# Cross-attention and lookup-table FFN: small DVE steps of the first score stage moved to GpSimd, and the way from batch 0 to batch 1 written in another order

## The chip, the cores and the metric

One core of a Trainium2 chip runs the whole program. The metric is the device time of one launch in microseconds (us). Engines are named as the profile names them: PE (TensorE), DVE (VectorE), ACT (ScalarE), POOL (GpSimd) and SP (SyncE, which here only issues DMAs).

## What is computed

For four batches of 512 rows of 512 numbers: a layer norm, cross-attention with 16 heads against a context, and an FFN whose weights are picked from a table of 16 numbers by integer indices. Cut to what matters:

```python
q = _ln((x @ Wq + bq).reshape(b, s1, H, HD), qn_w, qn_b)        # H = 16 heads of HD = 32
k = _ln(y_main @ Wk + bk, kn_w, kn_b);  v = y_main @ Wv + bv      # 496 keys of the context
k_dca = _ln((y_dca @ Wkv_dca + bkv_dca)[:, :, 0], ...)            # its last 16 rows
ctx = softmax(q @ k.T / sqrt(HD)) @ v + softmax(q @ k_dca.T / sqrt(HD)) @ v_dca
x = x + ctx @ Wo + bo                                            # after _layernorm(x)
gate, up = lut[gate_idx] , lut[up_idx]                           # 1376 x 512 indices each
h = jax.nn.silu(x_ @ gate.T) * (x_ @ up.T)                       # x_ = _layernorm(x)
out = x + h @ lut[down_idx].T
```

Everything is kept to about float32: each operand is split into an fp16 high half and an fp16 low half (`low = value - high`), and a product is three matmuls (high*high, high*low, low*high).

## The kernel before, in words

Every engine has a program written out by hand; semaphores tie them together, so the order of an engine's work is the order in the code. A batch goes through `core(a, ...)` on each engine. Its parts are: projections and head norms of eight (batch 0: nine) **units**, each 128 rows of queries ("q") or keys ("k", "d"); a **score stage** of 32 steps `m`, taken in 16 pairs; a short **shift** part; and a **value stage** of 16 steps. Between the steps of one batch, `between(slot)` runs pieces of the FFN of the batch before. Batch 0 has no batch before it; its slots are used for building the FFN weights.

**Building the weights.** The indices come as int32. POOL casts them to fp16, one block at a time (`convert(it)`, line 586), SP stores a block to a DRAM copy (`store_idx`) and loads each of its 33 chunks back replicated (`load_rep(c)`, line 403, three buffers `l_rep`). DVE compares a chunk with four index values in four **comparisons** (`one_hot(c)`, line 1007, 128x2048 fp16, into `l_oh`, four quarters). PE multiplies these by the table (`look_up(c)`, line 1570), which leaves a high half in bank FB and a low half in bank FB + 1. ACT copies both out (`lookup_out(c)`, lines 722 and 723), after which `l_out` frees the banks. Chunks 0 to 15 are compared in the score stage of batch 0, one per pair, and the rest in its value stage; chunks 31 and 32 are looked up in the slots `AHEAD` and `AHEAD + 1`, that is, after batch 1 has begun.

**Score stage of batch 0.** For each step DVE takes a maximum over two heads (line 1308, from PSUM), ACT takes exponentials in place (line 895), and PE computes the next pair of scores (line 1794) into one of three pairs of banks. After the maxima of a pair DVE makes the four comparisons of a chunk, and PE looks up the chunk before. From the seventh pair on PE also projects a tile of values or keys of batch 1 per pair into the same bank FB + 1 (`early(e)`, line 1519), which ACT copies out (lines 750 and 753). For each of the four query tiles DVE also does three small steps on the 16 extra keys: `dca_top` (maximum, 1145), `dca_shift` (add the negated maximum, 1149) and `dca_sum` (1153), with ACT's exponential `dca_exp` (938) between the last two. Three more DVE steps stand in or next to this stage: `low_half(7)` and `low_half(8)` (line 1133) and `context_lo` (line 1084).

**From batch 0 to batch 1.** PE projects batch 1's remaining query tiles, turns normalised heads by transposes (`turn_heads(u)`, line 1716), and computes batch 0's output rows (`out_rows`). DVE adds the residual (`residual(t)`, line 1078) from `x2`, which SP loads from `x` (line 476). It then takes the moments, normalises (`standardise`) and splits off the low half (`stage`, line 1066). ACT's `stage` (line 740) makes the high half. SP turns both halves by transposing DMAs (`turn`, lines 435 and 437). The FFN of batch 0 begins on PE in slot 4 and waits until all eight have landed. `variance(u)` (1111), POOL's `rstd(u)` (638) and `normalise(u)` (1121) make the head norm of unit u, from ACT's `square(u)` (764).

**Memory.** `arena` is one tile that is cut again for each stage. In front of the change `x2` (residual) lies on the comparison quarters 2 and 3 (`oh_late`) and the first replica.

## Time and profile before

| what | value |
|---|---|
| device time, three runs | 828.86, 830.95, 832.27 us (median 830.95) |
| profiled execution | 831.39 us |
| its span | 829.6 us |
| mean granted clock of PE | 0.981 |
| busy: PE, DVE, ACT, POOL | 765.0, 520.6, 491.2, 234.6 us |
| score stage of batch 0 | from the first maxima at 60.02 us to about 146 us |
| value stage of batch 0 | about 149 to 207 us |
| from batch 0 to batch 1 | about 207 to 259.5 us, when PE begins batch 1's scores |

PE's busy share over the whole span is 92%, but it is not even: in 60 to 91 us it is 18.16 of 31 us. So the table has to be read by stage. Where DVE is busy without a break and the others wait for it, a step taken from DVE counts; where PE is busy without a break, only PE's work counts. The time of 831.39 us is that of the execution whose trace is read here; it lies 0.44 us above the median.

### The profile page before, as it was taken

What the parts mean: (1) busy time and instruction counts of PE and PEld (TensorE: products, weight loads), DVE (VectorE), ACT (ScalarE), POOL (GpSimd) and SP (SyncE); (2) the same over time, 40 slices, a digit from 0 to 9 for tenths busy, and PEclk for the clock granted to TensorE, in tenths of its full rate; (3) what the DMA queues carried; (4) which work ended last, traced back from release to release, by engine and by line L of the source; (5) the groups of instructions that cost most, each with busy time, mean ns of one, the idle gap of its engine ahead of it and who ended that gap; (6) DMA issues with size and microseconds to landing.
All of it is one profiled execution on the core that took longest, in us unless ns stands there. A gap on an engine that the chain in (4) does not pass through costs nothing.

```text
span 829.6 us, 14807 instructions
## 1 busy us (share of the span) xinstructions
PE 765.0 (92%) x5842; PEld 313.0 (38%) x5842; DVE 520.6 (63%) x1007; ACT 491.2 (59%) x1000; POOL 234.6 (28%) x248
## 2 busy tenths in 40 slices
PE   3777676899989999999999999999999999999998
PEld 1342222233434334223543343234533332255445
DVE  7879999899866995223759972218589911053211
ACT  3477888888535886663648876644578856511100
POOL 6782111000842222003642220005622210013320
PEclk9998999899989999999999999999999999999999
DMA  7739697396330000321300002232000000000001
GB/s 247 185 101 269 186 262 211 105 194 147 127 79 1 1 1 14 77 58 58 79 0 2 1 1 51 64 86 49 8 1 2 2 26 26 27 26 1 0 13 39
DMA packets 73252, 58.60 MB, mean 71 GB/s; under 512 B 33312, under 2 KB 60704, under 8 KB 73056
## 3 DMA queue, kind: packets, MB, share of 16 engines
q1 hardware_dynamic: 72848, 57.40, 26.3%
q8 instruction: 46, 0.75, 0.4%
q10 hardware_dynamic: 208, 0.26, 0.2%
q14 instruction: 22, 0.18, 0.1%
q0 software_dynamic: 128, 0.00, 0.0%
HBM read 41.72 MB, written 9.50 MB: 62 GB/s over the span
## 4 chain that ended last, share of the span: by engine, by line
PE 75%; DVE 16%; ACT 4%; issue 2%; DMA 1%; POOL 0%; SPq 0%; DVEq 0%; ACTq 0%
PE ps L1519 50%; PE ps L1840 7%; PE ps L1821 6%; PE ps L1570 5%; DVE nmax L1311 3%; DVE nmax L1312 3%; PE ps L1794 3%; DVE arena L1007 2%; PE ps L1827 2%; PE ps L1716 2%; DVE arena L1014 2%; DVE nmax L1308 1%; ACT ps L895 1%; DMA arena<-in_Wq 1%; ACT wf_hi L722 1%
## 5 line engine op out<-in xcount | busy, mean ns | idle before, releaser
L1519 PE MATMUL ps<-arena,wf_hi 128*128 128x512 f16 (+2 forms) x736 | 212.8, 373 | 4.1 <-DVE arena L1014 3.0
L895 ACT ACTIVATE ps<-ps,nmax 128x496 f32<-128x496 f32 x256 | 166.2, 652 | 26.8 <-DVE nmax L1311 26.8
L925 ACT ACTIVATE arena<-ps 128x1024 f32<-128x1024 f32 x128 | 124.3, 1026 | 74.0 <-PE ps L1827 74.0
L1519 PE MATMUL ps<-arena,wf_lo 128*128 128x512 f16 (+2 forms) x368 | 136.8, 372 | 0.0
L1519 PE MATMUL ps<-wf_hi,arena 128*128 128x512 f16 (+3 forms) x374 | 114.8, 368 | 0.0
L638 POOL TENSOR_TENSOR hrstd<-hvar,mhalf 128x16 f32<-128x16 f32 (+1 forms) x33 | 98.5, 3001 | 47.1 <-DVE hvar L1111 47.0
L1519 PEld LDWEIGHTS ps<-arena,wf_hi 128*128 128x128 f16 (+1 forms) x736 | 69.8, 100 | 91.7 <-DVE arena L1014 13.1
L1007 DVE TENSOR_SCALAR arena<-arena,wf_lo 128x2048 f16<-128x2048 f16 (+1 forms) x132 | 89.1, 738 | 4.4 <-PE ps L1570 4.3
L614 POOL TENSOR_TENSOR xrstd<-xvar,mhalf 128x1 f32<-128x1 f32 x32 | 20.4, 638 | 211.9 <-DVE xvar L1049 211.9
L1570 PE MATMUL ps<-arena,wf_lo 128*32 128x512 f16 (+1 forms) x1056 | 66.0, 391 | 8.6 <-ACT arena L750 2.7
L1519 PE MATMUL ps<-wf_lo,arena 128*128 128x512 f16 (+3 forms) x187 | 68.5, 366 | 0.0
L1840 PE MATMUL ps<-arena 128*32 128x512 f32 x512 | 68.2, 604 | 0.0
L1794 PE MATMUL ps<-arena 32*128 32x512 f16 x768 | 53.6, 382 | 12.1 <-ACT ps L895 12.1
L1519 PEld LDWEIGHTS ps<-wf_hi,arena 128*128 128x128 f16 (+1 forms) x374 | 36.4, 97 | 73.3 <-issue 38.8
L1312 DVE TENSOR_REDUCE nmax<-ps 128x1 f32<-128x496 f32 x96 | 63.8, 665 | 0.0
L1311 DVE TENSOR_REDUCE nmax<-ps 128x1 f32<-128x496 f32 x96 | 63.8, 665 | 0.0
L543 POOL TENSOR_TENSOR idle<-mhalf 128x1 f32<-128x1 f32 x44 | 8.9, 203 | 193.6 <-DVE arena L1022 193.6
L1027 DVE SCALAR_TENSOR_TENSOR arena<-ps,arena 128x512 f32<-128x512 f32 x15 | 10.4, 692 | 84.9 <-PE ps L1519 84.9
L730 ACT ACTIVATE arena<-ps 128x512 f32<-128x512 f32 (+1 forms) x44 | 26.3, 598 | 61.2 <-PE ps L1519 61.2
L1014 DVE SCALAR_TENSOR_TENSOR arena<-arena,ps 128x512 f32<-128x512 f32 (+1 forms) x44 | 30.0, 682 | 44.5 <-ACT arena L730 44.5
L1821 PE MATMUL ps<-arena 32*128 32x512 f16 x768 | 53.5, 381 | 0.0
L895 ACT ACTIVATION_READ_ACCUMULATOR ps<-ps,nmax 128x1 f32 x256 | 53.3, 208 | 0.0
(147 smaller groups left out, 1040.2 us busy)
## 6 DMA issues: line engine op xcount, KB each, us to landing
arena<-idx SPq DMA_DIRECT2D x124, 128.0 KB, 3.3
arena<-in_x SPq DMA_DIRECT2D x32, 256.0 KB, 2.9
wf_lo<-in_idx SPq DMA_DIRECT2D x10, 512.0 KB, 5.4
idx<-wf_hi SPq DMA_DIRECT2D x10, 384.0 KB, 3.5
out<-arena SPq DMA_DIRECT2D x15, 256.0 KB, 2.0
wf_lo<-in_idx SPq DMA_DIRECT2D x11, 256.0 KB, 6.2
arena<-in_ctxT SPq DMA_DIRECT2D x4, 512.0 KB, 5.0
arena<-in_Wq SPq DMA_DIRECT2D x4, 256.0 KB, 6.4
```

The source lines that it names most:

```text
L638: pool.tensor_tensor(hrstd[0:n_, u % 2, :], hvar[0:n_, u % 2, :], mhalf[0:n_, :], ALU.pow).then_inc(s["hrstd_set"], 1)
L895: last = act.activation(sc, sc, ACT.Exp, bias=nmax[:, 0, t, h:h + 1], accum_out=den[:, 0, t, h:h + 1])
L925: act.activation(probs[n_ % 2][:, 2 * p:2 * p + 2, :], ps[:, bank:bank + 2, :], ACT.Exp).then_inc(s["probs_set"], 1)
L1007: dve.tensor_scalar(l_oh[q][:, 0:n_], l_rep[c % REPS][:, 0:n_], l_j[:, q:q + 1], None, ALU.is_equal)\
L1014: dve.scalar_tensor_tensor(out=g, in0=g, scalar=1.0, in1=ps[0:m, ffn_bank(f, it), :], op0=ALU.add, op1=ALU.mult)\
L1311: dve.tensor_reduce(nmax[:, 0, t, 2 * p:2 * p + 1], sc[:, 0:1, DCA:S], AX_X, ALU.max, negate=True).then_inc(s["max_set"], 1)
L1312: dve.tensor_reduce(nmax[:, 0, t, 2 * p + 1:2 * p + 2], sc[:, 1:2, DCA:S], AX_X, ALU.max, negate=True)\
L1519: last = pe.matmul(dst, l, r, start=(first and i == 0), stop=(stop and i == len(todo) - 1))
L1570: last = pe.matmul(ps[g * 32:(g + 1) * 32, FB + a_, 0:w], l_c[a_][:, q, :], l_oh[q][:, g * w:(g + 1) * w], start=(q == 0), stop=(q == NJ - ...
L1794: last = pe.matmul(ps[:, pair_bank(m + j // 2) + j % 2, :], qT[x_][of_head(j), g, cols], kT[y_][of_head(j), g, :], start=(k == 0), stop=(k ...
L1821: pe.matmul(ps[:, SC + j, :], kT[x_][of_head(j), g, cols], qT[y_][of_head(j), g, :], start=(k == 0), stop=False)
L1840: last = pe.matmul(ps[j * HD:(j + 1) * HD, pv_bank(g), :], v_sb[:, kt, h * HD:(h + 1) * HD], probs[n_ % 2][:, j, :], start=(kt == 0), stop ...
```

## The change

1. **POOL takes small steps of DVE in batch 0's score stage.** `low_half(7)`, `low_half(8)`, the low half of the early context (in two halves) and the shifts `dca_shift` of tiles 0, 1 and 2 are done by POOL, each placed between casts and made to wait for a count of finished comparisons. The fourth shift stays on DVE.
2. **ACT** takes `dca_exp` one step later (p = 4) and DVE `dca_sum` two steps later (p = 7) in batch 0. `lookup_out` copies the low half first and announces it by a new semaphore `l_free`; `early` waits for that alone.
3. **PE** computes the first pair of scores before `turn_heads(8)`.
4. **Memory:** the replicas `l_rep` come first, so that `x2` lies on replicas 0 and 1. SP loads the residual when the comparisons of chunk 31 are done, ahead of its reload of the values, and no longer after the last look-up.
5. **From batch 0 to batch 1** the order on DVE, ACT, PE and POOL is written anew: the last chunk's comparisons are split in two pairs around the first residual, squares and variances come earlier, and PE begins the FFN (slot 4) before `turn_heads(5)`.

```diff
@@ memory
         at[0] = a_x
-        oh_late = [wide() for _ in range(2)]
         l_rep = [wide() for _ in range(2)]
-        l_oh = [wide() for _ in range(2)] + oh_late
+        l_oh = [wide() for _ in range(2)]
+        x_first = [xs[0], xs[1]] + [arena[:, at[0] + i * D:at[0] + (i + 1) * D] for i in range(2)]
+        l_oh += [wide() for _ in range(2)]
@@ SP
+            sp.wait_ge(s["oh_set"], NJ * (NCH - 1))
+            first = residual_row(0)
+            for t in range(T):
+                load_residual(t, first)
             sp.wait_ge(s["pv_done"], G * T)
             sp.wait_ge(s["v_out"], 16 * T)
             sp.dma_start(v_sb.rearrange("p t n -> p (t n)"), v_next).then_inc(s["v_in"], 16)
-            sp.wait_ge(s["oh_used"], NJ * NCH)
...
@@ POOL
+            def low_half(u):
+                t = UNITS_0[u][1]
+                cols = slice(t * P, (t + 1) * P)
+                pool.wait_ge(s["tr_lo"], u)
+                pool.wait_ge(s["tr_hi"], u + 1)
+                pool.tensor_tensor(qT[1][:, :, cols], ys[u % 2].rearrange("p (g s) -> p g s", g=G), qT[0][:, :, cols],
+                                   ALU.subtract).then_inc(s["tr_lo"], 1)
+            def context_low(chunks):
+                pool.wait_ge(s["oh_set"], NJ * chunks)
+                pool.wait_ge(s["cT_hi"], 2)
+                for k in range(KC):
+                    last = pool.tensor_tensor(cT_early[1][:, k, :], ctx_early[:, k * S:(k + 1) * S], cT_early[0][:, k, :], ALU.subtract)
+                last.then_inc(s["cT_lo"], 1)
+            def dca_shift(t, chunks):
+                part = sd[:, t * H:(t + 1) * H, :]
+                pool.wait_ge(s["oh_set"], NJ * chunks)
+                pool.wait_ge(s["dca_max"], t + 1)
+                pool.tensor_tensor(part, part, nmax[:, 1, t, :].unsqueeze(2).to_broadcast([P, H, DCA]), ALU.add).then_inc(s["sd_set"], 1)
...
@@ ACT
-                act.activation(wf_hi[:, lo:hi], ps[:, FB, 0:hi - lo], ACT.Copy)
-                act.activation(wf_lo[:, lo:hi], ps[:, FB + 1, 0:hi - lo], ACT.Copy).then_inc(s["l_out"], 1)
+                act.activation(wf_lo[:, lo:hi], ps[:, FB + 1, 0:hi - lo], ACT.Copy).then_inc(s["l_free"], 1)
+                act.activation(wf_hi[:, lo:hi], ps[:, FB, 0:hi - lo], ACT.Copy).then_inc(s["l_out"], 1)
...
-                    if p == 3 and t:
+                    if p == (4 if prev is None else 3) and t:
                         dca_exp(a, t - 1)
@@ DVE
+                    one_hot(NCH - 1, (0, 1))
+                    residual(0, prev)
+                    moments(2, 0, prev, rows_of(0))
+                    one_hot(NCH - 1, (2, 3))
...
-                    if m == 1:
+                    if m == 1 and prev is not None:
                         low_half(len(units) - 1)
-                    if t and p == 2:
+                    if t and p == 2 and prev is not None:
                         dca_shift(t - 1)
-                    if t and p == 5:
+                    if t and p == (7 if prev is None else 5):
                         dca_sum(t - 1)
...
-                if slot == S_ONE + 6:
-                    context_lo((0, 1), ctx_early, cT_early)
@@ PE
-                pe.wait_ge(s["l_out"], EARLY_FROM + e - 1)
+                pe.wait_ge(s["l_free"], EARLY_FROM + e - 1)
...
                     scores(m)
+                    if prev is None and m == 0:
+                        turn_heads(8)
```

On DVE, at the seventh and eighth step of batch 0's score stage (before), with the low half of the context between two maxima:

```order
L1308 TENSOR_REDUCE nmax<-ps 128x2
L1084 TENSOR_TENSOR arena<-arena 128x1024
L1308 TENSOR_REDUCE nmax<-ps 128x2
L1007 TENSOR_SCALAR arena<-arena,wf_lo 128x2048 x4
```

The steps that POOL does from the second cast on, in the kernel after (lines 632 low half, 639 context, 646 shift, 587 casts):

```order
L587 CAST wf_hi<-wf_lo 128x1536
L632 TENSOR_TENSOR arena<-arena 128x4x128
L587 CAST wf_hi<-wf_lo 128x1536 x2
L632 TENSOR_TENSOR arena<-arena 128x4x128
L587 CAST wf_hi<-wf_lo 128x1536
L639 TENSOR_TENSOR arena<-arena 128x512 x2
L587 CAST wf_hi<-wf_lo 128x1536
L646 TENSOR_TENSOR arena<-arena,nmax 128x256
L587 CAST wf_hi<-wf_lo 128x1536 x2
L646 TENSOR_TENSOR arena<-arena,nmax 128x256
L587 CAST wf_hi<-wf_lo 128x1536 x2
L646 TENSOR_TENSOR arena<-arena,nmax 128x256
```

Before, the casts stand there alone, one after the other; seven elementwise steps now stand among them.

PE from batch 0's last output rows to the first FFN pieces, before (1519 products, 1716 turned heads; the products with `wq` are the projections of units 5, 6 and 7):

```order
L1716 MATMUL ps<-ident,arena 128x128 x4
L1519 MATMUL ps<-wq,arena 128x512 x12
L1519 MATMUL ps<-b,sel_q 128x512
L1519 MATMUL ps<-wq,arena 128x512 x12
L1519 MATMUL ps<-b,sel_q 128x512
L1519 MATMUL ps<-wq,arena 128x512 x12
L1519 MATMUL ps<-b,sel_q 128x512
L1716 MATMUL ps<-ident,arena 128x128 x4
L1519 MATMUL ps<-arena,wf_hi 128x512 x2
```

and after (1552 products, 1749 turned heads):

```order
L1552 MATMUL ps<-wq,arena 128x512 x12
L1552 MATMUL ps<-b,sel_q 128x512
L1749 MATMUL ps<-ident,arena 128x128 x4
L1552 MATMUL ps<-wq,arena 128x512 x12
L1552 MATMUL ps<-b,sel_q 128x512
L1552 MATMUL ps<-wq,arena 128x512 x12
L1552 MATMUL ps<-b,sel_q 128x512
L1552 MATMUL ps<-arena,wf_hi 128x512 x2
```

Unit 5 is projected before unit 4 is turned, and the first FFN products (`wf_hi`) follow the last projection at once; the turning of unit 5 comes after the pieces of slot 4.

## Rows read from the trace of the kernel before

**Rows 1.** Busy time by engine in four stretches; then clock, DMA share, GB/s.

```profile
60.00:91.00 31.00, 18.16 (x232) 5.62 (x232) 30.43 (x39) 24.28 (x71) 5.88 (x4) 0.83 0.88 242
91.00:131.00 40.00, 31.90 (x358) 11.44 (x359) 38.77 (x51) 33.27 (x98) 4.88 (x4) 0.96 0.88 232
149.00:207.00 58.00, 57.83 (x855) 20.80 (x856) 52.98 (x93) 49.08 (x71) 2.22 (x4) 0.97 0.71 155
240.00:242.00 2.00, 0.00 (x0) 0.00 (x0) 0.28 (x1) 0.00 (x0) 2.00 (x2) 0.74 0.38 69
```

**Rows 2.** Timeline of DVE in the score stage: start, length, operation, idle before.

```profile
58.78 1.25 DVE L1133 TENSOR_TENSOR arena<-arena 128x512 f16<-128x512 f32 x1 [0.34 <-ACT arena L786]
60.02 2.29 DVE L1308 TENSOR_REDUCE nmax<-ps 128x2 f32<-128x992 f32 x2
62.23 0.68 DVE L1133 TENSOR_TENSOR arena<-arena 128x512 f16<-128x512 f32 x1
...
76.92 1.23 DVE L1084 TENSOR_TENSOR arena<-arena 128x1024 f16<-128x1024 f32 x1 [0.57 <-ACT arena L744]
...
95.43 2.74 DVE L1007 TENSOR_SCALAR arena<-arena,wf_lo 128x2048 f16<-128x2048 f16 x4 [0.27 <-PE ps L1570]
...
138.46 2.73 DVE L1007 TENSOR_SCALAR arena<-arena,wf_lo 128x2048 f16<-128x2048 f16 x4
...
144.41 0.42 DVE L1149 TENSOR_TENSOR arena<-arena,nmax 128x256 f32<-128x256 f32 x1
```

**Rows 3.** Operations by shape in 56 to 150 us: the shifts and the small maxima.

```profile
L1149 DVE TENSOR_TENSOR arena<-arena,nmax 128x256 f32<-128x256 f32 x4 | 3.0, 751 | 0.0
...
L1145 DVE TENSOR_REDUCE nmax<-arena 128x16 f32<-128x256 f32 x4 | 1.6, 408 | 0.0
```

**Rows 4.** Timeline of POOL: casts in the score stage, and a later low half.

```profile
58.02 1.47 POOL L586 CAST wf_hi<-wf_lo 128x1536 f16<-128x1536 int32 x1
65.63 1.47 POOL L586 CAST wf_hi<-wf_lo 128x1536 f16<-128x1536 int32 x1 [6.13 <-DVE arena L1007]
...
253.47 1.16 POOL L609 TENSOR_TENSOR arena<-arena 128x512 f16<-128x512 f32 x1
```

**Rows 5.** Chain of waits through one pair with an early projection: start, length.

```profile
96.65 0.60 ACT wf_hi L722
97.25 0.49 ACT wf_lo L723
...
97.79 1.48 PE ps L1519 x6
...
99.94 1.94 PE ps L1570 x32
```

**Rows 6.** Timeline of ACT: copying out an early value, an early key.

```profile
99.29 0.60 ACT L750 ACTIVATE arena<-ps 128x512 f32<-128x512 f32 x1 [0.16 <-PE ps L1519]
...
120.76 0.60 ACT L753 ACTIVATE arena<-ps 128x512 f32<-128x512 f32 x1 [0.38 <-PE ps L1519]
```

**Rows 7.** Chain of waits where the FFN of batch 0 begins.

```profile
238.43 4.08 issue
242.51 1.09 PE ps L1716 x4
243.60 4.73 PE ps L1519 x12
...
248.76 2.59 PE ps L1519 x12
```

**Rows 8.** Timeline of DVE there: the third residual.

```profile
228.99 0.68 DVE L1078 SCALAR_TENSOR_TENSOR arena<-ps,arena 128x512 f32<-128x512 f32 x1
```

**Rows 9.** Timeline of SP's queue: the last transposing DMAs; and their time to landing.

```profile
235.53 1.19 SPq L435 DMA_TRANSPOSE arena<-arena  x1
...
239.39 1.26 SPq L437 DMA_TRANSPOSE arena<-arena  x1
...
DMA to landing us min/median/max: 2.5/2.5/4.0
```

More of the change, by code:

```diff
@@ L485, in _ @@
             sp.dma_start(v_sb.rearrange("p t n -> p (t n)"), v_next).then_inc(s["v_in"], 16)
-            sp.wait_ge(s["oh_used"], NJ * NCH)
-            first = residual_row(0)
-            for t in range(T):
-                load_residual(t, first)
             def store(f, t):
@@ L652, in core @@
                     rstd(3)
+                    norm(2, 0, prev)
                     rstd(4)
-                    for t in range(T):
+                    for t in range(1, T):
                         norm(2, t, prev)
@@ L1481, in between @@
                 def between(slot):
-                    if not sum(f) and slot == AHEAD:
-                        one_hot(NCH - 1)
                     for it in range(IT):
@@ L1766, in core @@
                     project_values(4)
-                    for u in range(6, 9):
-                        turn_heads(u)
+                    turn_heads(6)
+                    turn_heads(7)
                 elif sum(a) > 1:
```

93 lines of the change are left out of this document (53 added, 40 removed).

## The prediction, before the kernel was run

> **What bounds the kernel now.** I read the busy times by stage first, because the shares over the whole span hide what matters. In 60 to 91 us DVE is busy 30.43 of 31 us and PE only 18.16; in 91 to 131 us DVE has 38.77 of 40 us; in 149 to 207 us PE has 57.83 of 58 us [rows 1]. So the first score stage is bound by DVE, its second half almost equally by something else, and the value stage behind it by PE, where nothing of this change can gain. Then I read DVE's timeline in the score stage. It is a plain alternation: two maxima (2.29 us in the row, the next step starts 2.21 us later), four comparisons (2.74 us, of which about 0.09 lies under the next step, so 2.65), and now and then an extra step [rows 2]. A pair of steps without extras is 2.20 + 2.65 = 4.85 us. The extras are what the change takes away. Then I read the chain of waits from 91 to 131 us. It does not stay on DVE: it runs look-up on PE (1.94), high half out (0.60), low half out (0.49), early projection on PE (1.48), copying that out on ACT (0.60), next look-up [rows 5, 6]. DVE waits for PE there, 0.27 us before the comparisons at 95.43 [rows 2]. Last, the chain of waits behind the value stage: PE stands still from 238.43 for 4.08 us, and what it does next, at 243.60, takes 4.73 us for the same 12 products that take 2.59 us at 248.76 [rows 7]. The granted clock falls in between (0.74 as a mean of 240 to 242 us, so it changed from the upper to the lower level near 241 us) [rows 1].
>
> **Start of the score stage.** Before, the first maxima start at 60.02, behind `low_half(7)`, which starts at 58.78 and takes 1.25 us, because POOL's cast from 58.02 to 59.49 runs beside it; the same step takes 0.68 us at 62.23 with no cast beside it [rows 2, 4]. Now POOL has that step, and PE computes the first scores before it turns unit 8. These scores need POOL's copies of the extra keys, which stand just before the cast at 58.02 [rows 4], so about 58.1; a first score pair is ready some 0.85 us later. I set the first maxima at 58.95: 1.07 us earlier.
>
> **First six pairs, up to the comparisons that started at 95.43.** Before that is 95.43 - 60.02 = 35.41 us [rows 2]. Now there are seven times two maxima (7 x 2.20), six times four comparisons (6 x 2.65) and one `dca_top` (the row says 408 ns, with its overlap taken off 0.33) [rows 3]: 15.40 + 15.90 + 0.33 = 31.63 us. The gain is 3.78 us. It checks against the parts: `low_half(8)` 0.60, `context_lo` 1.15 and its wait of 0.57, one shift 0.75 less its overlap, one `dca_sum` 0.33 that moves behind this point, and the wait of 0.27. With the start, the seventh chunk's comparisons begin 4.85 us earlier.
>
> **Next eight pairs, 95.43 to 138.46.** Before that is 43.03 us, two shifts among them; all four shifts average 751 ns but the one with no cast beside it takes 0.42 us [rows 2, 3]. DVE alone would now need 8 x 4.85 and four small steps of 0.33 = 40.1 us. The other loop needs more. In it ACT waits 0.16 us before it copies out an early value and 0.38 us before an early key [rows 6]; that is all that the low-half-first order can give, since ACT does the same two copies and the exponentials either way. From the end of one look-up to the end of the next is 0.03 + 0.60 + 0.49 + 0.05 + 1.48 + 0.02 + 0.61 + 0.04 + 1.94 = 5.26 us [rows 5, 6]; it becomes 5.10, and with keys, whose loop is 0.22 longer before, 5.10 too. `dca_exp`, moved to where ACT waits for the look-up, is hidden. Eight pairs of 5.10 are 40.8 us: 2.2 us less.
>
> **Taken off again.** POOL's new steps must fit beside the maxima. A low half costs POOL 1.16 us [rows 4]; the context is two such, 2.32; a shift is half the size and not shown on POOL, so its bounds are 0.58 (half of that row) and 1.16; I take 0.7. Each stands behind a count of comparisons, and the maxima last 2.20 us. Only one place overruns: cast and low half together are 1.47 + 1.16 = 2.63 us, 0.43 more than the two maxima. If the overrun stops the comparison it costs 0.43. Does a POOL step slow a maximum? The maxima beside the cast at 65.63 do not stretch: the second pair of DVE, 65.48 to 67.68, has the same 2.20 us. The bounds for the seven steps together are then 0 and 7 x 0.4 = 2.8 us (0.4 is what a cast costs a shift). I take 0.3, nearest to the row with the maxima.
> A rule of the Trainium skill speaks against the change here: "SBUF — State Buffer", section "Who interferes with whom", says that VectorE and GpSimd share a pair of ports as an exclusive lock, taken by a comparison of this kind (`tensor_scalar` in a two-port mode) or by two SBUF inputs against a GpSimd read, but never by a `tensor_reduce`. The stretched shifts and low half agree, and so do the unstretched maxima. By the rule the sum would lose the overrun of 0.43 us, by the rows 0.3.
> Score stage in all: 1.07 + 3.78 + 2.2 - 0.3 = 6.75 us. The value stage is PE work without a gap, so it only starts earlier and passes this on.
>
> **From batch 0 to batch 1** (times in the old clock of the trace). PE's work up to 238.43 is the same list in another order and has almost no gap before; I give it nothing. It resumes when the transposing DMAs have landed. Before, the third tile's first transpose starts at 235.53, the last at 239.39, and it lands 2.5 us after its start: 241.9 [rows 9]. PE resumed later still, at 242.51 [rows 7], for a head norm of unit 5. Now DVE's list up to the third residual is shorter in waits: the residual is loaded long before, and stepping the new order through with the row lengths (0.6 per 512-wide step, 1.32 for two comparisons, 1.1 for moments) puts that residual at about 227.0 where it was 228.99 [rows 8]. From there to the third tile's first transpose there are 5.7 to 6.5 us of steps, so it starts at 233 to 233.7, and the last landing is 6.4 us later, at 239.5 to 240.2. I take 240.1. The FFN pieces run first and `turn_heads(5)` behind them, with the same total, so PE is 242.51 - 240.1 = 2.4 us earlier. The head norm of unit 5 is ready at about 239.5 (variance 5 is taken before the last `stage`, some 2.9 us earlier) and the pieces cover it.
> The stop is then 238.4 to 240.1, shorter than the 2.6 us after which the clock fell. If the clock stays at 2.4 GHz, PE saves 4.73 - 2.59 = 2.14 us on the 12 products and, by the same factor 1.83, 0.5 to 0.65 us on the four transposes (1.09 us before): 2.8 us [rows 7]. Bounds: 0 and 2.8; I take 2.8, since the fall near 241 us lies behind the new start.
>
> **Cost at nothing, and its cover.** The residual's 1 MB now goes ahead of the reload of the values; that reload is first used by batch 1's value stage, over 100 us later. ACT's square of unit 5 waits for a projection of PE, but stands before a `stage` whose input comes later. DVE now waits for the last look-up before its first `standardise` of batch 0; queued behind it are the whole norm chain and the transposes. The look-up ends at about 222.8 and DVE gets there at about 223.4; if PE were later by more than 0.6 us, everything behind slides with it.
>
> **Sum.** 6.75 + 2.4 + 2.8 = 11.95 us off the profiled 831.39, which gives 819.4. That execution lies 0.44 above the median of 830.95, so against the median it would be 819.0. I predict 819.4, with its own range 817 to 822.
>
> **Rivals.**
> *The clock falls all the same* between the batches (the stop of PE is only shortened, to some 1.8 us, and a later landing lengthens it). Then the 2.8 us stay lost: 822.2. For it: the margin to 241 us is under 1 us. Against it: the fall came 2.6 us into the stop.
> *The replica loads take over in the score stage.* The DMA engines have a share of 0.88 at 242 GB/s in 60 to 91 us [rows 1]. The same bytes in 31 - 4.3 us would ask for 0.88 x 31 / 26.7 = 1.02. Against it: DVE waits for no load in the whole stage, and three replica buffers let a load be late by almost a pair. If it takes over, half of the 6.75 us goes: 822.8; with the clock falling too, 825.6.
> *POOL holds up the comparisons*: at its upper bound, 2.8 instead of 0.3 us, 821.9. For it: a cast beside a shift or a low half nearly doubled each [rows 2, 3]. Against it: the waits on counts keep all but one of POOL's steps beside maxima.
> *The gain is not there*: the chain in 91 to 131 us holds at its old 5.26 us a pair and more, and the order between the batches gives nothing, so only the first pairs gain: 831.4 - 4.5 = 826.9, within 0.5% of before.
> *Slower*: the early projections run at the lower clock. The first one already does so at 91 us, when PE has stood and waited. If PE stays at 1.2 GHz through the eight pairs, look-up and projection cost 1.6 and 1.2 us more (the 12 products of [rows 7] show a factor 1.83), a pair is 5.10 + 2.8 = 7.9 us, eight pairs lose 22.4 us, and the end is at 841.8. It outweighs all gains from the fifth such pair on. For it: PE is busy only 18.16 of 31 us before. Against it: the clock was 0.96 in 91 to 131 us, and PE has the same work in less time now.
>
> **Numbers.** Forecast 0.52, clock 0.16, loads 0.14, POOL 0.07, no gain 0.07, slower 0.04. A measurement of this kernel tells a change from none at about 0.5%, that is 4.2 us: under 826.8 is faster, over 835.1 slower. Faster is 0.52 + 0.16 + 0.14 + 0.07 = 0.89 and a part of the case without gain, 0.02; same 0.05; slower 0.04. The range for 8 in 10 is 815.5 to 826: it holds the forecast, the clock, loads and POOL, and below it a somewhat larger saving between the batches.
>
> **What would show it.** In the profile after: first maxima at about 59.0; pairs of 4.85 us up to the sixth comparison group, then 5.10, with DVE waiting for PE and the wait of ACT before lines 750 and 753 gone; the last comparisons of the stage some 6.8 us earlier; POOL's low halves at 1.16 us and no comparison group longer than 2.74; the residual's DMA at about 203.6 on the new clock; PE's stop between the batches under 2 us and 12 FFN products in 2.59 us right after it; batch 1's first scores at about 259.5 - 11.95 = 247.5. If the comparisons stretch, the POOL step is wrong; if PE's stop is still over 3 us, the step on the transposes is.

## The result, and the profile after

The kernel after takes 820.46 us (median of four runs, 819.84 to 822.64) where the kernel before takes 829.92 us beside it (four runs, 828.86 to 832.27): a ratio of 0.9887, 95% interval 0.9856 to 0.9918. So it is 9.5 us faster. The forecast was 819.4 us, its range 815.5 to 826. The profiled execution after is the longest of its four, 822.64 us with a span of 820.5; before it was 831.39 and 829.6.

How much comes from where is best read at four marks that every kernel of this study has: POOL's copies of the extra keys (in front of the first scores), PE's transposes at the end of the score stage (`caug`), the look-up of chunk 31, and batch 1's first scores. All stages are differences of such starts.

| stretch, us | before | after | gained | forecast |
|---|---|---|---|---|
| to the copies of the extra keys | 57.67 | 58.48 | -0.81 | 0 |
| to the transposes (score stage) | 91.01 | 85.36 | 5.65 | 6.75 |
| to the look-up of chunk 31 (value stage) | 64.09 | 65.21 | -1.12 | 0 |
| to batch 1's first scores | 46.72 | 41.34 | 5.38 | 5.2 |
| to the end of the span | 570.11 | 570.11 | 0.00 | 0 |

The sum is 9.10 us, the difference of the two spans. So the forecast of 11.95 us was right in its two large terms to within 1.1 us, and two terms that it did not have took 1.9 us off. (Below it is shown that these two are the granted clock of single executions, and no effect of the change.)

Busy times by stage after (stretch and its length, then busy time with count of PE, PE's weight loads, DVE, ACT and POOL; granted clock, DMA share, GB/s):

```profile
60.00:91.00 31.00, 20.88 (x242) 6.87 (x240) 30.86 (x38) 26.98 (x78) 11.28 (x10) 0.78 0.96 260
91.00:131.00 40.00, 32.93 (x414) 12.17 (x418) 40.00 (x52) 35.27 (x105) 7.00 (x5) 1.00 0.92 242
240.00:242.00 2.00, 2.00 (x13) 1.10 (x12) 1.35 (x4) 0.75 (x2) 0.09 (x1) 1.00 0.00 0
```

Beside [rows 1]: DVE was busy 38.77 of 40 us in the second stretch and is now busy all 40.00; POOL has the work that DVE gave away; the transfers moved from 0.88 to 0.96 of the DMA engines' time in the first stretch; and the clock in 240 to 242 us is 1.00 where it was 0.74 (PE is at work again by then; in its stop, in 234 to 236 us, the clock is 1.00 too). DVE's timeline after (start, duration, instruction, count; in brackets the idle time ahead and what ended it), against [rows 2]:

```profile
59.93 2.29 DVE L1345 TENSOR_REDUCE nmax<-ps 128x2 f32<-128x992 f32 x2 [0.67 <-PE ps L1829]
62.13 2.73 DVE L1043 TENSOR_SCALAR arena<-arena,wf_lo 128x2048 f16<-128x2048 f16 x4
...
69.86 2.28 DVE L1345 TENSOR_REDUCE nmax<-ps 128x2 f32<-128x992 f32 x2
72.06 3.07 DVE L1043 TENSOR_SCALAR arena<-arena,wf_lo 128x2048 f16<-128x2048 f16 x4
...
114.93 2.28 DVE L1345 TENSOR_REDUCE nmax<-ps 128x2 f32<-128x992 f32 x2
117.12 0.41 DVE L1189 TENSOR_REDUCE den<-arena 128x16 f32<-128x256 f32 x1
117.45 3.93 DVE L1043 TENSOR_SCALAR arena<-arena,wf_lo 128x2048 f16<-128x2048 f16 x4
121.30 2.28 DVE L1345 TENSOR_REDUCE nmax<-ps 128x2 f32<-128x992 f32 x2
```

The alternation of maxima and comparisons is what the forecast drew, with no wait shown behind the first row. Two comparison groups stick out: 3.07 and 3.93 us where the others take 2.73 (one more, at 107.28, takes 2.88). POOL's timeline says what ran beside them:

```profile
71.44 1.15 POOL L632 TENSOR_TENSOR arena<-arena 128x512 f16<-128x512 f32 x1
...
106.16 1.47 POOL L587 CAST wf_hi<-wf_lo 128x1536 f16<-128x1536 int32 x1 [9.24 <-DMA wf_lo<-in_idx]
110.24 0.62 POOL L646 TENSOR_TENSOR arena<-arena,nmax 128x256 f32<-128x256 f32 x1 [2.61 <-DVE arena L1043]
117.52 1.99 POOL L587 CAST wf_hi<-wf_lo 128x1536 f16<-128x1536 int32 x1 [6.66 <-DMA wf_lo<-in_idx]
```

The low half follows a cast and reaches 0.5 us into the comparisons of 72.06: the one overrun that was foreseen. The cast of 117.52 was not: it had waited 6.66 us for its indices from a DMA, and when they came, it started into the middle of a comparison group. Both suffer, the cast 1.99 instead of 1.47 us and the group 3.93 instead of 2.73.

The chain of waits through two early projections, in the same execution:

```profile
91.21 1.94 PE ps L1603 x32
...
93.18 0.60 ACT wf_lo L756
93.77 0.49 ACT wf_hi L757
...
94.35 1.30 ACT ps L931 x4
95.66 0.50 ACT arena L784
...
96.19 1.94 PE ps L1603 x32
```

This is the loop of PE and ACT as it runs after the change: look-up, both copies, ACT's exponentials of a step, and the early value copied out, 4.98 us from one look-up to the next. The projection is no longer in it; it ends before ACT is through with its exponentials. PE's look-ups start at 91.21, 96.19, 101.18, 106.16, 111.14, 116.13 and 121.11 us, values and keys alike, while DVE's groups are now 4.84 and now 5.17 us apart. In index_first below, where no cast disturbs DVE, the eight pairs from the seventh group take 40.07 us, 5.01 each. So both loops are within 0.03 us a pair of each other: DVE isn't seen waiting, but by these numbers taking more from it alone would gain next to nothing here.

Behind the value stage, the third residual, two of the transposing DMAs, and the chain of waits (start, duration, what), against [rows 7], [rows 8] and [rows 9]:

```profile
222.47 0.69 DVE L1114 SCALAR_TENSOR_TENSOR arena<-ps,arena 128x512 f32<-128x512 f32 x1
```

```profile
229.59 1.19 SPq L436 DMA_TRANSPOSE arena<-arena  x1
...
233.44 1.26 SPq L438 DMA_TRANSPOSE arena<-arena  x1
```

```profile
234.46 1.57 issue
236.03 2.75 PE ps L1552 x12
238.78 0.44 PE ps L1749 x4
239.22 2.59 PE ps L1552 x12
```

PE stands 1.57 us where it stood 4.08, resumes 2.59 us after the start of the last transpose (2.5 was the landing time read before), and its 12 products take 2.75 us where they took 4.73.

### The profile page after: what moved, and what is told of

It is laid out like the page before. It is cut to its first block, busy times and chain, and to the rows that moved or that the text cites. A ratio compares the mean times of both kernels' runs of the same rounds, so it can differ in the third digit from the quotient of the medians.

```text
span 820.5 us, 14816 instructions
## 1 busy us (share of the span) xinstructions
PE 763.7 (93%) x5842; PEld 313.0 (38%) x5842; DVE 517.3 (63%) x1001; ACT 490.5 (60%) x1000; POOL 239.4 (29%) x255
## 4 chain that ended last, share of the span: by engine, by line
PE 74%; DVE 18%; ACT 3%; issue 3%; POOL 1%; DVEq 0%; POOLq 0%; ACTq 0%
PE ps L1552 49%; PE ps L1877 8%; PE ps L1858 6%; PE ps L1603 5%; DVE arena L1043 3%; DVE nmax L1348 3%; DVE nmax L1349 3%; PE ps L1829 3%; DVE nmax L1345 2%; PE ps L1864 2%; DVE arena L1050 2%; PE ps L1749 2%; ACT ps L931 1%; POOL hrstd L660 1%; DVE arena L1347 1%
## 5 line engine op out<-in xcount | busy, mean ns | idle before, releaser
L1043 DVE TENSOR_SCALAR arena<-arena,wf_lo 128x2048 f16<-128x2048 f16 (+1 forms) x132 | 91.1, 752 | 4.0 <-PE ps L1603 3.7
L1603 PE MATMUL ps<-arena,wf_lo 128*32 128x512 f16 (+1 forms) x1056 | 68.8, 406 | 9.5 <-ACT arena L784 3.6
```

Of the source, the lines that this page charges most:

```text
L1043: dve.tensor_scalar(l_oh[q][:, 0:n_], l_rep[c % REPS][:, 0:n_], l_j[:, q:q + 1], None, ALU.is_equal)\
L1603: last = pe.matmul(ps[g * 32:(g + 1) * 32, FB + a_, 0:w], l_c[a_][:, q, :], l_oh[q][:, g * w:(g + 1) * w], start=(q == 0), stop=(q == NJ - ...
```

## The experiments

There are three groups: score_only to lfree_only, residual_early to ungated, and the last three. Each group ran on one chip beside runs of the kernel before of its own (medians 830.58, 831.12 and 830.52 us), and the ratios are to these. All times but the first are medians. The stages are those of the table above, from each kernel's profiled execution.

| kernel | us | ratio to before, 95% | copies at | score | value | between |
|---|---|---|---|---|---|---|
| before | 831.39 (traced) | | 57.67 | 91.01 | 64.09 | 46.72 |
| after | 820.46 | 0.9887 (0.9856 to 0.9918) | 58.48 | 85.36 | 65.21 | 41.34 |
| score_only | 826.03 | 0.9942 (0.9930 to 0.9955) | 57.38 | 87.77 | 65.30 | 45.81 |
| between_only | 826.85 | 0.9954 (0.9942 to 0.9966) | 57.23 | 90.90 | 65.20 | 41.32 |
| pool_only | 828.77 | 0.9980 (0.9969 to 0.9991) | 58.53 | 87.26 | 64.29 | 46.84 |
| lfree_only | 830.54 | 0.9999 (0.9987 to 1.0011) | 55.69 | 90.74 | 64.13 | 45.92 |
| residual_early | 823.97 | 0.9912 (0.9897 to 0.9927) | 57.39 | 85.74 | 64.80 | 44.77 |
| ffn_after_turn | 819.91 | 0.9863 (0.9847 to 0.9880) | 57.39 | 84.30 | 64.50 | 40.86 |
| index_first | 819.99 | 0.9872 (0.9850 to 0.9893) | 57.63 | 84.17 | 63.91 | 41.32 |
| ungated | 821.30 | 0.9886 (0.9865 to 0.9906) | 57.25 | 87.61 | 65.16 | 41.32 |
| full_again | 820.81 | 0.9884 (0.9869 to 0.9899) | 55.70 | 86.99 | 63.86 | 41.32 |
| index_first_again | 820.55 | 0.9889 (0.9872 to 0.9905) | 58.62 | 84.01 | 64.47 | 41.32 |
| combined_turn | 818.68 | 0.9860 (0.9844 to 0.9877) | 55.69 | 84.55 | 64.95 | 41.06 |

From batch 1's first scores to the end every one of these executions takes 569.98 to 570.15 us. The copies lie between 55.69 and 58.62 us without regard to the kernel (before 57.67, the same full change 58.48 and 55.70), and the value stage, whose code is alike in all, takes 63.86 to 65.30. So -0.81 and -1.12 us of the first table are within what executions differ by, not effects of the change.

The traces also show what the executions differ in: the granted clock behind a stop of PE. Ahead of the score stage, after a stop of about 3 us, PE does 12 products with `wv`. The same kernel in two executions, after and full_again:

```profile
27.92 5.28 PE L1552 MATMUL ps<-wv,arena 128*128 128x512 f16 x12 [3.28 <-DVE arena L1120]
...
27.93 2.75 PE L1552 MATMUL ps<-wv,arena 128*128 128x512 f16 x12 [3.27 <-DVE arena L1120]
```

Their granted clock in 25 to 35 us is 0.66 and 1.00. All 13 executions fall into three groups by that number: at 1.00 (three of them) the copies come at 55.69 to 55.70 us, at 0.83 (seven, before among them) at 57.23 to 57.67, at 0.66 (three) at 58.48 to 58.62. The value stage has the same in small. Its first look-up, behind the transposes that end a stop of 4.9 to 6.8 us, again in after and full_again:

```profile
146.18 3.60 PE L1603 MATMUL ps<-arena,wf_lo 128*32 128x512 f16 x32
...
145.03 2.25 PE L1603 MATMUL ps<-arena,wf_lo 128*32 128x512 f16 x32
```

In the kernel before it takes 2.48 us, 1.12 less than in after: the whole of the -1.12 us. Without that look-up the stage takes 61.59 to 61.69 us in ten of the 13 executions, and up to 62.05 in the rest.

### The two halves apart

Parts 1 to 3 of the change alone (score_only), and parts 4 and 5 alone (between_only). The mark lines of each:

```diff
 score_only
+                    low_half(7)
+                    context_low(4)
+                    dca_shift(0, 6)
+                    if prev is None and m == 0:
+                        turn_heads(8)
 between_only
+            for t in range(T):
+                load_residual(t, first)
+                    one_hot(NCH - 1, (0, 1))
+                    residual(0, prev)
+                    one_hot(NCH - 1, (2, 3))
```

> Parts 1 to 3 of the change alone (POOL takes low halves, context and three shifts; low half of a look-up out first; first scores before the last turned unit); memory and the order between the batches as before. Theory, that the change is two independent gains added up: the last comparisons of the stage start 5 to 5.8 us earlier than in the kernel before when both are counted from POOL's copies of the extra keys, about 1 us of that is lost again to the first look-ups of the value stage running at the lower clock, and the time is 3.7 to 5 us below before (ratio 0.994 to 0.9955). PE still stops for about 4 us before the first FFN pieces. Rival, that the stage is tied to the transfers and only the new order between the batches pays: less than 2 us (ratio over 0.9975).

> Parts 4 and 5 alone (memory, early residual, the new order from batch 0 to batch 1); the score stage as before. Theory of independent gains: PE's stop before the first FFN pieces is 1.5 to 2 us instead of 4.1, the 12 products behind it take 2.6 to 2.8 us instead of 4.7, and from the look-up of chunk 31 to batch 1's first scores there are 41.3 us instead of 46.7; the time is 5.2 to 5.5 us below before (ratio 0.9935). This and the run with parts 1 to 3 should add up to the whole, 9.3 us (ratio 0.9887). Rival, that the early start of the score stage is needed for the clock to stay up: the stop is short but the 12 products take over 4 us, and the gain is 2.5 to 3 us (ratio 0.9965).

score_only gains 4.55 us against the 830.58 of before on its chip, between_only 3.73; together 8.3 where the whole change gave 9.5 against its own. The first is in the range expected; the second misses it by 1.5 us, though its stop (1.56 us), its products (2.75) and its way are as expected. Parts 1 to 3 shorten the score stage, parts 4 and 5 only the way between the batches (46.72 to 41.32, the full 5.4 us, with the old score stage in front). Neither effect needs the other. (The way of score_only is 0.91 us shorter than before although its stop is the same 4.08 us: its 12 products took 3.63 us in place of 4.73, by the clock.) Its score stage gained only 3.24 us where the last comparisons were expected 5 to 5.8 us earlier, because three casts met comparisons. The first two, in its DVE timeline:

```profile
76.20 3.93 DVE L1039 TENSOR_SCALAR arena<-arena,wf_lo 128x2048 f16<-128x2048 f16 x4
...
82.58 2.73 DVE L1039 TENSOR_SCALAR arena<-arena,wf_lo 128x2048 f16<-128x2048 f16 x4
...
87.43 3.93 DVE L1039 TENSOR_SCALAR arena<-arena,wf_lo 128x2048 f16<-128x2048 f16 x4
```

and its POOL timeline:

```profile
77.25 1.67 POOL L586 CAST wf_hi<-wf_lo 128x1536 f16<-128x1536 int32 x1 [5.71 <-DMA wf_lo<-in_idx]
80.22 2.27 POOL L638 TENSOR_TENSOR arena<-arena 128x512 f16<-128x512 f32 x2 [1.29 <-DVE arena L1039]
87.99 1.50 POOL L586 CAST wf_hi<-wf_lo 128x1536 f16<-128x1536 int32 x1 [5.50 <-DMA wf_lo<-in_idx]
```

The context's low half of 80.22, which waits for a count of comparisons, hurts nothing; both casts had waited for a DMA. The third group, of 3.90 us, starts at 118.80 with a cast from 118.70 beside it.

### POOL's steps without the earlier low half, and the reverse

pool_only has the steps on POOL and the later exponential and sum, and neither `l_free` nor the earlier scores (its edit is part 1 and 2 of the diff shown with the change, without the lines on `l_free`). lfree_only has only this:

```diff
-                act.activation(wf_hi[:, lo:hi], ps[:, FB, 0:hi - lo], ACT.Copy)
-                act.activation(wf_lo[:, lo:hi], ps[:, FB + 1, 0:hi - lo], ACT.Copy).then_inc(s["l_out"], 1)
+                act.activation(wf_lo[:, lo:hi], ps[:, FB + 1, 0:hi - lo], ACT.Copy).then_inc(s["l_free"], 1)
+                act.activation(wf_hi[:, lo:hi], ps[:, FB, 0:hi - lo], ACT.Copy).then_inc(s["l_out"], 1)
...
-                pe.wait_ge(s["l_out"], EARLY_FROM + e - 1)
+                pe.wait_ge(s["l_free"], EARLY_FROM + e - 1)
```

> Only the steps given to POOL, with the later sum and exponential; the high half of a look-up still goes out first, the early projections wait for both halves, and the last unit is turned before the first scores. Theory, that the gain of the score stage is DVE's removed work and that DVE is then just as slow as the loop of PE and ACT: eight pairs from the seventh comparison group on keep 5.26 us (values) and 5.47 us (keys), 42.9 us in all with DVE waiting for PE again by 0.2 to 0.6 us a pair, so the time is 2 to 3.5 us below before (ratio about 0.9965). Rival, that the order of the two copies does nothing: the same eight pairs take 41.4 us as in the full change, and the time is that of parts 1 to 3 within 0.5 us.

> Only ACT's order: low half of a look-up out first, announced by its own semaphore, and the early projections wait for that alone. DVE keeps all its steps. Theory, that DVE bounds the stage when it keeps its extras: DVE's waits for PE in the stage (1.2 us) go and nothing else, so the time is 0.5 to 1.2 us below before (ratio about 0.999). Rival, that the copy order itself is the gain of the score stage: 2 to 4 us below before.

pool_only gains 1.8 us, a little less than the least expected. With DVE relieved and the old order of ACT's copies, the other loop binds. DVE in pool_only waits for the look-up in five pairs of eight:

```profile
108.72 2.74 DVE L1039 TENSOR_SCALAR arena<-arena,wf_lo 128x2048 f16<-128x2048 f16 x4 [0.32 <-PE ps L1599]
111.38 2.28 DVE L1339 TENSOR_REDUCE nmax<-ps 128x2 f32<-128x992 f32 x2
114.19 2.74 DVE L1039 TENSOR_SCALAR arena<-arena,wf_lo 128x2048 f16<-128x2048 f16 x4 [0.53 <-PE ps L1599]
```

These two groups are 5.47 us apart, the loop of an early key; with values it is 5.26, the length read from [rows 5] and [rows 6]. The eight pairs take 42.52 us, 42.9 expected. With `l_free` the loop is 4.98 us, as the chain of the kernel after shows, 0.12 less than the forecast's 5.10. lfree_only takes DVE's waits away too, but leaves DVE its steps, and its score stage is only 0.27 us shorter; one group of 3.93 and one of 3.37 us, beside late casts, hold 1.84 us that before doesn't have. Its time (0.04 us below before, 0.5 to 1.2 expected) can't be told from before. So the earlier low half alone is not shown to be worth anything. Beside POOL's steps, and together with the earlier scores, it is worth 2.7 us by the medians (826.03 against 828.77); the two traced score stages don't show it (87.77 against 87.26), since score_only's holds three groups of 3.9 us.

### The residual's load without the new order

residual_early has parts 1 to 4 (the memory and the early load) and the old order of part 5. Beside it, ffn_after_turn has all, but PE turns unit 5 ahead of the first FFN pieces, as before (ACT's and DVE's neighbouring steps go with it). Against the kernel after, on DVE in residual_early and on PE in ffn_after_turn:

```diff
 residual_early
-                    one_hot(NCH - 1, (0, 1))
-                    one_hot(NCH - 1, (2, 3))
-                    dve.wait_ge(s["oh_used"], NJ * NCH)
+                        one_hot(NCH - 1)
 ffn_after_turn
+                    turn_heads(5)
                     between(4)
-                    turn_heads(5)
```

> The full change without its new order between the batches (part 5): the score stage of the change and its memory, so that the residual is loaded when chunk 31 is compared and no longer after the last look-up; every engine's order between the batches as before. Theory, that the order and not the early load makes the gain there: DVE's wait of 0.9 us for the residual goes, PE still stops for 3 to 4 us for the head norm of unit 5 and the products behind it run at the lower clock; the time is 0.3 to 1 us below parts 1 to 3 alone and 4.5 to 5 us above the full change. Rival, that the late residual was what held the chain: the stop falls under 2.5 us and the time comes within 2 us of the full change.

> The full change, but unit 5 is turned before the first FFN pieces on PE, and ACT and DVE take the pieces of slots 4 to 8 in the place that they had before. Theory, that the stop of PE is now set by the transposing DMAs (they land at about 236.0 in the changed kernel, 1.57 us after PE's last projection) and that the head norm of unit 5 is ready before: unit 5's heads are ready at 235.1, so PE turns them inside the stop and the FFN starts at the same time; the time is the full change's, or 0.4 us below it. Rival, that putting the FFN first is what shortened the stop: PE stops for unit 5 until later than 236.5, and the time is over 1 us above the full change.

The chain of waits of residual_early:

```profile
233.29 3.35 issue
236.64 0.90 PE ps L1746 x4
237.53 4.00 PE ps L1549 x12
```

The stop is 3.35 us, and 12 products still take 4.00, where 2.59 is their length at the upper level of 2.4 GHz: a part of them ran at 1.2 GHz. Against score_only (45.81 between the batches) the early load gives 1.0 us and the new order another 3.4 (44.77 to 41.34), of which 1.8 are the shorter stop and the rest the clock (0.90 + 4.00 against 2.75 + 0.44). The time of residual_early, 823.97 us, is 7.2 us below before where the full change has 9.5 and 9.7 (full_again); the distance of 4.5 to 5 us that was expected to the full change did not come. With the heads turned first (ffn_after_turn) the way is 40.86, no longer than with the FFN first. So that swap is not what makes part 5 gain; by the traces it loses 0.5 us, and the median of 819.91 can't tell.

### POOL's steps not tied to comparisons

ungated leaves out the two waits for a count of comparisons in front of POOL's context and shifts:

```diff
             def context_low(chunks):
-                pool.wait_ge(s["oh_set"], NJ * chunks)
                 pool.wait_ge(s["cT_hi"], 2)
...
             def dca_shift(t, chunks):
                 part = sd[:, t * H:(t + 1) * H, :]
-                pool.wait_ge(s["oh_set"], NJ * chunks)
                 pool.wait_ge(s["dca_max"], t + 1)
```

> The full change, but POOL's shifts and its low half of the early context no longer wait for a count of comparisons; they start when their inputs are ready, that is beside comparisons and no longer beside maxima. Theory, that POOL and DVE hold each other up when a comparison meets a POOL step but not when a maximum does (a cast that met comparisons in the changed kernel took 1.99 us instead of 1.47, and the comparisons 3.93 instead of 2.74): each shift lengthens a comparison group by 0.3 to 0.6 us and the context by up to 2.3, DVE's four-comparison groups sum to 2 to 4 us more, and the time is 1 to 3.5 us above the full change. Rival, that the cast's case was something else: no group is longer, and the time is the full change's within 0.3 us.

Its score stage takes 87.61 us, with groups of 3.95, 3.59 and 3.49 us. On DVE and on POOL:

```profile
76.53 3.95 DVE L1041 TENSOR_SCALAR arena<-arena,wf_lo 128x2048 f16<-128x2048 f16 x4
...
107.81 3.59 DVE L1041 TENSOR_SCALAR arena<-arena,wf_lo 128x2048 f16<-128x2048 f16 x4
```

```profile
75.90 2.71 POOL L638 TENSOR_TENSOR arena<-arena 128x512 f16<-128x512 f32 x2
...
108.47 1.06 POOL L644 TENSOR_TENSOR arena<-arena,nmax 128x256 f32<-128x256 f32 x1
```

The first group has nothing beside it but the context's low half, and pays 1.22 us. The other two have a late cast and behind it a shift, which takes 1.06 us instead of 0.62. By what a cast costs elsewhere (see the last section) the shift's part is about 0.36 us in each: an estimate of 1.9 us in all for the missing waits in this execution, near the low end of what was expected. The executions with the waits take 84.30 to 87.77, and the longest of them, score_only, has three groups of 3.9 as well, all from late casts. The time of 821.30 can't be told from the full change, where 1 to 3.5 us more was expected. So the traces show that the waits do what they are for; what they are worth in time stays open.

### The index block ahead of the replica

The full change's stage differs from execution to execution: score_only, after, residual_early, ffn_after_turn and full_again have the same steps in it and take 84.30 to 87.77 us. If late index blocks are the cause of the long groups, an earlier load ends them. From chunk 7 on SP stores and reloads the block before it loads the replica, and no longer behind it:

```diff
             for c in range(REPS, NCH):
+                ahead = c >= 7 and c % 2 and (c + 1) // 2 < IT
+                if ahead:
+                    store_idx((c + 1) // 2)
                 load_rep(c)
...
-                if c % 2 and (c + 1) // 2 < IT:
+                if c % 2 and (c + 1) // 2 < IT and not ahead:
                     store_idx((c + 1) // 2)
```

> The full change, but from the seventh chunk on SP stores and reloads an index block before it loads the next replica, no longer behind it, so that the index loads are issued about 1.7 us earlier. Theory, that one cast met comparisons only because its index block landed late (POOL waited 6.7 us for that load): the casts start beside maxima again, the group of 3.93 us is 2.74, and the last comparisons of the stage start 1.2 to 1.4 us earlier; the time is 1 to 1.4 us below the full change. Rival, that the earlier index loads only push the replicas back and DVE waits for those: DVE waits for a replica at least once and the time is the full change's or more.

> The full change once more, on the same chip and in the same rounds as the next two runs, as their yardstick. From its own first measurement: ratio 0.9887 to the kernel before, so about 820.5 us if the kernel before takes 830. The index load's lateness moves from execution to execution, so the theory of the late index load expects that some comparison group takes 3.9 us here too, though perhaps not at 117.45 us: two or more groups over 3.2 us, or one of 3.9 us. The rival, that the group of 3.93 us in the first trace was an accident of that execution, expects none above 3.1 us but the one beside the low half.

> The index block stored and reloaded ahead of the replica load, once more, now beside the full change. The theory that late index loads cost about 1.2 us of comparisons and some later time at the lower clock expects 1.5 to 3.5 us less than the full change on this chip (ratio between the two of 0.996 to 0.998). The rival, that the casts' collisions are a detail of the traced execution and that the difference between the first runs was chip and chance, expects the two within 0.8 us of each other.

In both traces of index_first, and in that of combined_turn, only the group beside the low half is longer than 2.9 us in the stage. From the first one:

```profile
114.09 2.27 DVE L1348 TENSOR_REDUCE nmax<-ps 128x2 f32<-128x992 f32 x2
116.29 0.40 DVE L1192 TENSOR_REDUCE den<-arena 128x16 f32<-128x256 f32 x1
116.61 2.73 DVE L1046 TENSOR_SCALAR arena<-arena,wf_lo 128x2048 f16<-128x2048 f16 x4
```

```profile
114.23 1.47 POOL L590 CAST wf_hi<-wf_lo 128x1536 f16<-128x1536 int32 x1 [4.21 <-DVE arena L1046]
```

The cast now waits for DVE's comparisons and starts with the maxima. The stage takes 84.17 and 84.01 us: 6.84 and 7.00 us less than before, where the forecast said 6.75. full_again, beside it, had groups of 3.60 and 3.49 us and 86.99. One more loss stands there, which no other trace with `l_free` shows: the early projection at 87.38 takes 2.43 us instead of 1.48 at a mean granted clock of 0.79 (84 to 92 us), as the first one of the kernel before did (2.74 us), and DVE waits for what follows:

```profile
91.54 2.74 DVE L1043 TENSOR_SCALAR arena<-arena,wf_lo 128x2048 f16<-128x2048 f16 x4 [0.62 <-PE ps L1603]
```

The projection, from PE's timeline of full_again:

```profile
87.38 2.43 PE L1552 MATMUL ps<-wv,arena 128*128 128x512 f16 x6 [0.18 <-ACT wf_lo L756]
```

So the cause of the long groups is shown. The time is another matter: index_first_again and full_again, on one chip, take 820.55 and 820.81 us, where 1.5 to 3.5 us were expected. In the traced executions the gain of 2.98 us in the score stage met copies that came 2.92 us later and a value stage that was 0.61 longer. The copies are the clock again (0.66 against 1.00 in 25 to 35 us), and 0.39 of the 0.61 are the first look-up. With four timed runs each, spread over 1.2 and 2.8 us, a gain of 1 to 2 us can't be shown; it isn't refuted either.

### Two edits together

combined_turn is index_first with the heads turned first, both as above.

> Two edits on top of the full change: index block ahead of the replica, and the heads of unit 5 turned before the first pieces of the FFN, as in the kernel before. The trace of the run with the turn first shows the same sum of stops (0.71 and 0.18 us in place of 1.57), so the theory expects at most 0.7 us from the second edit and 2 to 3.5 us less than the full change in all, about 817.5 to 818.5 us. If both edits of the earlier runs gave their 0.5 to 2 us independently, it is the fastest of the three; the rival, that each only moved the time within its uncertainty, expects all three within 0.8 us.

It is the fastest kernel of the study: 818.68 us, and its four runs (818.50 to 818.97) lie all below the four of the full change on the same chip (820.11 to 821.26). Against before the ratio is 0.9860, interval 0.9844 to 0.9877. The gain of 2.1 us over the full change is in the range expected. Its chain of waits:

```profile
230.60 1.27 issue
231.86 0.63 PE ps L1751 x4
232.49 2.59 PE ps L1554 x12
```

Since index_first alone gave nothing that can be told on this chip, how the 2.1 us divide between the edits stays open. And since the clock ahead of the score stage alone moves an execution by up to 2.9 us, four runs that agree within 0.5 us may owe part of their lead to it; only one of them is traced.

## Why the prediction was right, and where not

- *What bounds the score stage.* Right for the kernel before and for the first pairs: DVE. From the seventh pair on the forecast expected PE and ACT to bind and DVE to wait for PE, and that sign did not come: DVE's waits are gone and its busy share in 91 to 131 us is 40.00 of 40.
- *Start of the stage*, 1.07 us. Right, once both traces are set to the copies of the keys: first maxima 2.35 us behind them before, 1.45 after, so 0.90 us.
- *First six pairs*, 3.78 us. Nearly right: 32.17 us where 31.63 were forecast, so 3.24 gained. 0.34 of the difference is the overrun of the low half, which the forecast had in another term; some 0.2 stand in the first pair, of 5.08 us.
- *Pairs of 4.85 us.* Right: 4.84 to 4.85 for pairs without extras. *The other loop at 5.10 us* is 4.98 us long. The forecast took only ACT's short wait off the old chain; in fact the chain takes another way, over ACT's exponentials. So the eight pairs are DVE's own: without disturbance they take 40.07 us (index_first), where the forecast had computed 40.1 for DVE alone and then taken the 40.8 of the loop. In the kernel after they took 41.42 us from 92.10 to 133.52 (43.03 before), 1.20 of it for one late cast and 0.15 for another. Two errors of opposite sign, 0.7 and 1.35 us, made the forecast of 40.8 look closer than it was.
- *POOL's price*, 0.3 us with 0.43 for the overrun: right for the steps that were moved, though its sign "no group longer than 2.74" contradicted its own overrun. The shift takes 0.62 us on POOL (0.7 taken), the low half 1.15 (1.16), and beside it the group takes 0.34 us more. The term was too small all the same, because it counted only POOL's new steps. A cast that had waited for its block cost 1.2 us in this execution, and in the four other traces with these steps there are none to three groups of 3.2 us and more. That is the term that was mis-sized: the stage gained 5.65 us (3.2 to 6.7 in the five executions) for 6.75. The rival on the loads named the right queue and the wrong victim: no maximum, comparison or look-up waited for a replica, but the index block, which SP sends behind a replica, often no longer arrives in time for its place beside the maxima. (At the old pace it can be late too: lfree_only and between_only have such groups.) The waits after have this row for it (waiter, releaser: us in total, times, longest), where before had 18.6 us in two places:

```profile
POOL wf_hi L587 <- DMA wf_lo<-in_idx: 27.9, 4, 9.2
```

- The rule that was weighed there, the Trainium skill's "SBUF — State Buffer", section "Who interferes with whom" (an exclusive lock of VectorE and GpSimd, taken by a two-port `tensor_scalar` and never by a `tensor_reduce`), is borne out by these rows: maxima beside a cast or a low half keep 2.28 us, comparisons stretch. Where a cast falls wholly into a group, the measured price is 1.20 us, less than the cast's own 1.47 that a full block would cost; there the measurement decides. It would have charged each late cast, had its lateness been foreseen.
- *Between the batches*, 2.4 + 2.8 us. Right: 5.38. The third residual starts 13.4 us behind the look-up of chunk 31 where it started 16.2 [rows 8], the last transpose lands at 235.9 and PE resumes at 236.03; the forecast for this point, moved to the new clock, was 236.4. The stop is 1.57 us (1.7 forecast), and the clock holds: 2.75 for 4.73 us. It holds in all six traces with this order and a stop of 1.6 us or so. residual_early shows the other side of the same step: with a stop of 3.35 us the clock falls.
- *The slower rival* had the eight pairs at the lower clock. The granted clock is 1.00 in 91 to 131 us after. Of its mechanism full_again shows one case, with 0.62 us of DVE's time.
- *Two terms that it did not have*, -0.81 in front of the copies and -1.12 in the value stage, are the clock of single executions, as shown above; the traced execution of after had the slow case in both places. They would account for most of the 2.2 us by which it is above the median, but the other executions have no trace.
- *Luck.* The median is within 1.1 us of the forecast, but the gain is not: 9.5 us between the medians for 11.95. The forecast took its sum off the one traced execution of before, 831.39 us, which is 1.5 us above the median of 829.92; that closed more than half of the gap.

## What to carry to other kernels

Moving small steps to an idle engine pays when they start beside work that they don't disturb, and a wait on a count secures that only for the steps that have it: after a change of pace, look again at the steps that were there already and at which transfer they wait for. A stop of the matmul engine costs twice where its clock falls with it, so 2.5 us less of waiting made the way 5.4 us shorter. When the step that binds has been relieved, read the next loop from the new chain and not from the old one less a wait. And judge a stage by marks within one trace: here executions of one kernel differ by 3 us ahead of the stage that is in question. The granted clock of a stretch behind a stop of PE says which case an execution had.

## What was not expected of the hardware

- A cast of 128x1536 on POOL beside comparisons of 128x2048 fp16 on DVE takes 1.50 to 2.05 us instead of 1.47 when it starts within the group, and the four comparisons 3.93 instead of 2.73: the group pays 1.20 us, most of the cast's own length. The length of 3.93 comes back five times in four executions (after, score_only, residual_early, lfree_only). When POOL's step is already under way as the group begins, POOL keeps its length and the group pays the overlap less about 0.2 us: for overlaps of 0.35, 0.53, 0.84, 1.07 and 1.36 us it paid 0.15, 0.34, 0.64, 0.87 and 1.17 (after, lfree_only, full_again, score_only).
- The copies ahead of the first scores come at 55.7 to 58.6 us in executions of nearly the same code before them, while the last 570 us of the program repeat to within 0.17. The same stop of PE of 3.27 or 3.28 us is followed by a granted clock of 1.00, 0.83 or 0.66 in 25 to 35 us, and by 12 products of 2.75, 4.28 to 4.44 or 5.28 us.
- Stops of PE and what follows: after 1.57 us 12 products take 2.75 us, after 3.35 us 4.00, after 4.08 us 3.63 (score_only) and 4.73 (before). By the granted clock in stretches of 2 us (0.74 in 240 to 242 before; 0.51 there in score_only; 0.71 in 236 to 238 in residual_early) the fall came 2.5, 3.7 and 3.5 us behind the start of the stop: equal stops did not bring an equal fall.
